# Rounded parts made on GpSimd from one fp32 copy, and ScalarE's copies moved between two exponentials

## The chip, the cores and the metric

The kernel runs on 1 core of one Trainium2 chip. The metric is the device time of one execution in microseconds, the median of several.

## The reference

The input x has 16 images (batch entries) of 512 tokens by 256 features, in fp32. Per image:

```python
x = x + attn(layernorm(x))      # 16 heads of 16, softmax over 512 keys, biases
x = x + (round_fp8(clip(layernorm(x) / input_scale)) * input_scale) @ (w_fp8 * weight_scale).T + bias

# attn(x):
qkv = x @ qkv_w.T + qkv_b
scores = q @ k.T / 4
out = softmax(scores) @ v
return out @ proj_w.T + proj_b
```

## The kernel before, in words

Wherever fp32 accuracy is wanted of the faster fp32r matmuls, an operand is split into a high part (its value rounded to fp32r) and a low part (the value minus the high part), and the product is the sum of three matmuls over the pairs high-high, high-low, low-high. That holds for x (`xnT_p`, the transposed normalised x), q and k (`parts`), the attention output (`oT_p`) and the weights.

The work runs in slots of 32 steps (`STEPS`). In slot u the engines work on four images at once: image u is normalised, transposed and projected; for image u-1 the plain scores and their row maxima are made; for image u-2 the transposed scores, the exponentials and the product with v; for image u-3 the output projection, the second layernorm, the fp8 rounding and the linear layer. `present(n)` says whether image u-n exists. Each engine has its own instruction queue, written out step by step by the same loop, and works it strictly in order; semaphores tie the queues together. Slots 2 to 15 have images u, u-1 and u-2; from slot 3 also image u-3.

On TensorE every step issues: `scores_t(.., 0)` (bank `ps_t[:, 0]`, L455), `scores(.., 1)` (L469), `scores_t(.., 1)`, `scores(.., 0)`, then what the step has extra, and in odd steps eight matmuls with v (`values`, L487). Here t0 and t1 are the two transposed score matmuls, s1 and s0 the plain ones. The extras: v projection at steps 4 and 6 (L380), output projection at 8 and 10 (L406), transposes of x at 12 and 14 (L353), q/k projection at 16, 18, 20 and 22 (L369), transpose of the maxima at 5 and 25 (L390), transposes of the fp8 tile at 26 (L420), linear layer at 28 and 30 (L437). All of the extras use the one PSUM bank `ps_m`; `take_bank` makes TensorE wait for the reader of its last user. The wait of t0 and t1:

```python
if past(2 * STEPS * b + 2 * s + g - 1):
    pe.wait_ge(exp_done, 2 * STEPS * b + 2 * s + g - 1)
```

So t0 of a step needs the first exponential of the step before, and t1 the second. On ScalarE a step has the two exponentials (L566), and behind them the copies that the step's extras need: `copy_v` (L574), `copy_xnT` (L583 rounded, L586 fp32), `copy_oT` (L593) at steps 6 and 24, `copy_qk` (L602 rounded, L603 fp32, both with the bias) and `copy_hqT` (L609). `xnT` is a single buffer of one half of x, so its second fp32 copy waits for `xnT_low` of the first.

VectorE takes the maximum of each step's scores (L684), splits the transposed maxima (L729, L731), does layernorm sums, transposes of the attention output and back (L739, L750), reciprocals, and parts of the fp8 rounding (L765, L771). GpSimd does in this order in a slot: `layernorm_x`, `out_divide(.., 3)`, `low_oT(.., 1)`, `low_xnT(.., 0)` (L903), `out_divide(.., 0)`, `low_xnT(.., 1)`, `layernorm_h` (L939 to L951), `split` 0 and 1 (L924), `out_divide(.., 1)` (L933), `round_fp8` and `add_linear_bias`, `split` 2, `low_oT(.., 0)`, `split` 3, `out_divide(.., 2)`, `add_bias`. The SP queue issues the transfers, among them `stack`: twelve per image and head half, which lay the q and k parts into `qs` and `ks` for the next slot, after `low_ready`.

Of the kernel before, what the change touches and what calls it, by code (L numbers as in the profile page):

```python
# [7 lines left out]
F32R = mybir.dt.float32r  # L8
U32 = mybir.dt.uint32
ALU = mybir.AluOpType  # L10
ACT = mybir.ActivationFunctionType
# [31 lines left out]
PROJECT_V = (4, 6)  # L43
PROJECT_OUT = (8, 10)
TRANSPOSE_X = (12, 14)
PROJECT_QK = (16, 18, 20, 22)
TRANSPOSE_MAX = (25, 5)
TRANSPOSE_HQ = 26
# [3 lines left out]
COPY_OT = (24, 6)  # L52
# [8 lines left out]
def block_kernel(nc, x, qkv_wT, qk_bT, v_bT, proj_wT, proj_b, lin_wT, lin_b, in_scale, w_scale, eye, out):  # L61
# [4 lines left out]
    with ExitStack() as ctx:  # L66
        def sb(name, shape, dt=F32):
            return ctx.enter_context(nc.sbuf_tensor(name, shape, dt))

        def ps(name, shape):  # L70
            return ctx.enter_context(nc.psum_tensor(name, shape, F32))

        def sem(name):
            return ctx.enter_context(nc.semaphore(name))
# [24 lines left out]
        xnT = sb("xnT", [P, S])  # L99
        xnT_p = sb("xnT_p", [P, 2, NC, S], F32R)  # L100
        parts = sb("parts", [P, 2 * NT, 2, S])
# [35 lines left out]
        ps_t = ps("ps_t", [P, 2, S])  # L137
        ps_s = ps("ps_s", [P, 2, 2, S])
        ps_o = ps("ps_o", [P, S])
        ps_m = ps("ps_m", [P, S])  # L140
# [22 lines left out]
        v_done = sem("v_done")  # L163
# [31 lines left out]

        rs1_ready = sem("rs1_ready")
        xn_ready = sem("xn_ready")
        xnT_low = sem("xnT_low")
        oT_low = sem("oT_low")
        low_ready = sem("low_ready")  # L200
        res_ready = sem("res_ready")
        rs2_pow = sem("rs2_pow")
# [7 lines left out]
        def past(count):  # L210

            return not isinstance(count, int) or count > 0

        def run_slots(eng, slot, finish, prepare=None):

            def present(u):
                return lambda behind: 0 <= u - behind < B
            for u in range(NSLOT - 1):  # L220
                slot(u, u % 2, present(u))
                if u == 0 and prepare:
                    prepare()
            finish(B - 1)
# [332 lines left out]
        @block.scalar  # L557
        def _(act):
            def exps(b, s, a):
                n, w = s // 4, s % 4  # L560
                if w == 0 and a == 0 and past(UNITS * b + n - 1):
                    act.wait_ge(pv_done, UNITS * b + n - 1)
                if isinstance(b, int) and b == 0 and s == 0:
                    act.wait_ge(const_v, 9)
                act.wait_ge(st_done, 2 * (STEPS * b + s) + a + 1)
                nc.scalar.activation(pt[n % 2][:, w % 2 + 2 * a, w // 2, :], ps_t[:, a, :], ACT.Exp, scale=SCALE).then_inc(exp_done, 1)  # L566

            def copy_v(b, par, half):
                act.wait_ge(v_done, 2 * b + half + 1)
                if isinstance(b, int) and b == 0:  # L570
                    act.wait_ge(ones, 3)
                if past(UNITS * (b - 1)):
                    act.wait_ge(pv_done, UNITS * (b - 1))
                nc.scalar.copy(vt[par][:, 2 * half:2 * half + 2, :, 0:HD],  # L574
                               ps_m[:].rearrange("p (j h e) -> p j h e", j=2, h=H)).then_inc(v_ready, 1)

            def copy_xnT(b, c):

                bank = ps_t[:, c, :] if isinstance(b, int) and b == 0 else ps_m[:]
                act.wait_ge(xt_done, 2 * b + c + 1)  # L580
                if past(b):
                    act.wait_ge(v_done, 2 * b)
                nc.scalar.copy(xnT_p[:, 0, c, :], bank)  # L583
                if past(2 * b + c):
                    act.wait_ge(xnT_low, 2 * b + c)
                nc.scalar.copy(xnT[:], bank).then_inc(xnT_ready, 1)  # L586

            def copy_oT(b, t):

                act.wait_ge(oT_ready, NT * b + t + 1)  # L590
                if past(b):
                    act.wait_ge(proj_done, 2 * b)
                nc.scalar.copy(oT_p[:, 0, t, :], oT[:]).then_inc(oT_high, 1)  # L593

            def copy_qk(b, par, n):

                t, bias = n // 2, b_qk[:, (n % 2) * NT + n // 2:(n % 2) * NT + n // 2 + 1]
                bank = ps_s[:, n // 2, n % 2, :] if isinstance(b, int) and b == 0 else ps_m[:]
                act.wait_ge(qk_done, 4 * b + n + 1)
                if past(b):  # L600
                    act.wait_ge(stacked[t][1 - par], 96 * (b - 2 + par) + 192)
                nc.scalar.activation(parts[:, n, 0, :].bitcast(F32R), bank, ACT.Identity, bias=bias)  # L602
                nc.scalar.activation(parts[:, n, 1, :], bank, ACT.Identity, bias=bias).then_inc(whole_ready, 1)  # L603

            def copy_hqT(b):
                act.wait_ge(xq_done, b + 1)
                if past(b):
                    act.wait_ge(lin_done, 2 * b)
                nc.scalar.copy(hqT[:].rearrange("p c n -> p (c n)"), ps_m[:].bitcast(BF16)).then_inc(hqT_ready, 1)  # L609

            def slot(u, par, present):
                for s in range(STEPS):
                    if present(2):
                        exps(u - 2, s, 0)
                        exps(u - 2, s, 1)
                    if s == COPY_OT[1] and present(3):
                        copy_oT(u - 3, 1)
                    if s == COPY_OT[0] and present(2):
                        copy_oT(u - 2, 0)
                    if s in PROJECT_V and present(1):  # L620
                        copy_v(u - 1, 1 - par, PROJECT_V.index(s))
                    if s in TRANSPOSE_X and present(0):
                        copy_xnT(u, TRANSPOSE_X.index(s))
                    if s in PROJECT_QK and present(0):
                        copy_qk(u, par, PROJECT_QK.index(s))
                    if s == TRANSPOSE_HQ and present(3):
                        copy_hqT(u - 3)

            def finish(b):
                copy_oT(b, 1)  # L630
                for half in range(2):
                    act.wait_ge(xq_done, b + half + 1)
                    if half == 0:
                        act.wait_ge(lin_done, 2 * b)
                    nc.scalar.copy(hqT[:, :, 2 * half * P:2 * (half + 1) * P],
                                   ps_t[:, half, :].bitcast(BF16)[:, 0:S].rearrange("p (c n) -> p c n", c=NC)
                                   ).then_inc(hqT_ready, 1)


            act.wait_ge(half_set, 1)  # L640
            nc.scalar.activation(table[:], half_neg[:, 0:1], ACT.Exp)
            act.wait_ge(ident_in, 32)
            run_slots(act, slot, finish)

        @block.vector
# [236 lines left out]
        def _(pool):  # L882
# [16 lines left out]
            def low_xnT(b, c):  # L899
                pool.wait_ge(xnT_ready, 2 * b + c + 1)  # L900
                if past(b):
                    pool.wait_ge(v_done, 2 * b)
                pool.tensor_tensor(xnT_p[:, 1, c, :], xnT[:], xnT_p[:, 0, c, :].bitcast(F32),  # L903
                                   ALU.subtract).then_inc(xnT_low, 1)

# [15 lines left out]
            def split(b, n):  # L921

                pool.wait_ge(whole_ready, 4 * b + n + 1)
                pool.tensor_tensor(parts[:, n, 1, :], parts[:, n, 1, :], parts[:, n, 0, :],  # L924
                                   ALU.subtract).then_inc(low_ready, 1)

# [41 lines left out]
            def slot(u, par, present):  # L968
# [6 lines left out]
                if present(0) and later:  # L975
                    low_xnT(u, 0)
                if present(2):
                    out_divide(u - 2, 0)
                if present(0) and later:
                    low_xnT(u, 1)  # L980
                if present(3):
                    layernorm_h(u - 3)
                if present(0) and later:
                    split(u, 0)
                    split(u, 1)
# [5 lines left out]
                if present(0) and later:  # L991
                    split(u, 2)
# [59 lines left out]
```

## Time and profile before

| | |
|---|---|
| median of 3 runs | 1080.2 us (1075.93 to 1088.58) |
| the profiled execution | 1080.5 us, of which span 1078.7 us |
| TensorE busy | 975.6 us, 90% |
| VectorE busy | 857.8 us, 80% |
| ScalarE busy | 707.2 us, 66% |
| GpSimd busy | 465.6 us, 43% |
| granted TensorE clock, mean | 0.951 |

The span runs from the first instruction to the last. Busy shares are means over the whole span; matmuls are pipelined, and their ends in the profile are modelled, so starts are the safer reading. The granted clock is a share of full speed, 2.4 GHz. Times in the rows below count from the start of the span.

### The profile page before, as it was taken

The numbers are of one execution on the slowest core, as the hardware profiler recorded it, in microseconds if no ns is written. First come the engines' busy times: TensorE is split into PE (matmuls) and PEld (weight loads), VectorE is DVE, ScalarE is ACT, GpSimd is POOL, SyncE is SP. The second block draws the span as 40 slices with busy tenths as digits, with TensorE's granted clock in tenths as the row PEclk, the third lists the DMA queues.
The fourth block names the chain that finished last, engine by engine and source line by source line (L and its number), as shares of the span: only waits on it lengthen the run. The fifth ranks groups of instructions, "written<-read, shape, count | busy, mean of one in ns | idle before, by whom it ended". The sixth has DMA issues, their size and how long they took to land.

```text
span 1078.7 us, 16257 instructions
## 1 busy us (share of the span) xinstructions
PE 975.6 (90%) x5796; PEld 451.3 (42%) x5796; DVE 857.8 (80%) x1186; ACT 707.2 (66%) x1299; POOL 465.6 (43%) x443
## 2 busy tenths in 40 slices
PE   3487999999999999999999999999999999998894
PEld 2243334454444434444444444344444434443333
DVE  3576788888987888898988888888989888888216
ACT  3023767777685777777686777777686777766650
POOL 3121234627272463717264453727273553524242
PEclk9666999999998999999999999999999999999966
DMA  4928181745646083665638182645647181741000
GB/s 137 124 35 88 39 110 30 104 76 81 99 56 103 29 107 65 85 95 73 107 43 124 28 107 58 94 85 80 99 53 107 26 106 29 101 59 41 2 29 30
DMA packets 44288, 79.39 MB, mean 74 GB/s; under 512 B 9904, under 2 KB 13104, under 8 KB 44208
## 3 DMA queue, kind: packets, MB, share of 16 engines
q1 hardware_dynamic: 44208, 78.36, 48.5%
q8 instruction: 46, 0.75, 0.4%
q14 instruction: 34, 0.28, 0.1%
HBM read 18.42 MB, written 8.39 MB: 25 GB/s over the span
## 4 chain that ended last, share of the span: by engine, by line
PE 74%; ACT 14%; DVE 6%; issue 2%; DMA 2%; SPq 1%; POOL 1%; ACTq 0%; DVEq 0%; POOLq 0%
PE ps_t L455 27%; PE ps_o L487 18%; PE ps_m L369 9%; ACT pt L566 6%; PE ps_m L380 5%; PE ps_m L406 4%; PE ps_s L469 4%; ACT parts L602 4%; ACT parts L603 3%; DVE mx L684 3%; PE ps_m L437 2%; PE ps_m L353 2%; DMA ks<-parts 1%; PE ps_m L420 1%; DVE nm L700 1%
## 5 line engine op out<-in xcount | busy, mean ns | idle before, releaser
L684 DVE TENSOR_REDUCE mx<-ps_s 128x2 f32<-128x1024 f32 x512 | 616.6, 1215 | 112.4 <-PE ps_s L469 108.8
L566 ACT ACTIVATE pt<-ps_t 128x512 f32<-128x512 f32 x1024 | 558.9, 600 | 213.8 <-PE ps_t L455 205.6
L455 PE MATMUL ps_t<-qs,ks 50*128 50x512 f32 x1024 | 424.4, 474 | 44.3 <-ACT pt L566 39.1
L469 PE MATMUL ps_s<-ks,qs 48*128 48x512 f32 x1024 | 413.1, 482 | 23.6 <-DVE mx L684 12.1
L455 PEld LDWEIGHTS ps_t<-qs,ks 50*128 50x128 f32 x1024 | 168.5, 187 | 386.1 <-ACT pt L566 307.2
L487 PE MATMUL ps_o<-pt,vt 128*32 128x512 f32 x2048 | 277.7, 615 | 0.2 <-ACT pt L566 0.2
L469 PEld LDWEIGHTS ps_s<-ks,qs 48*128 48x128 f32 x1024 | 162.8, 190 | 37.6 <-DVE mx L684 19.4
L903 POOL TENSOR_TENSOR xnT_p<-xnT,xnT_p 128x512 fp32r<-128x512 f32 x30 | 38.3, 1277 | 212.7 <-ACT xnT L586 212.7
L933 POOL TENSOR_TENSOR on<-ot,rden 128x256 f32<-128x256 f32 x63 | 39.4, 626 | 174.8 <-DVE rden L743 174.8
L369 PE MATMUL ps_m<-xnT_p,wqkv_p 128*128 128x512 f32 x360 | 103.2, 423 | 1.5 <-POOL xnT_p L903 0.8
L924 POOL TENSOR_TENSOR parts<-parts 128x512 f32<-128x512 f32 x60 | 76.6, 1277 | 37.4 <-ACT parts L603 37.4
L602 ACT ACTIVATE parts<-ps_m,b_qk 128x512 fp32r<-128x512 f32 x60 | 41.3, 688 | 65.5 <-PE ps_m L369 65.5
L369 PEld LDWEIGHTS ps_m<-xnT_p,wqkv_p 128*128 128x128 f32 x360 | 65.3, 195 | 28.9 <-issue 14.9
L487 PEld LDWEIGHTS ps_o<-pt,vt 128*32 128x32 f32 x2048 | 40.6, 108 | 78.6 <-issue 73.5
L910 POOL TENSOR_TENSOR oT_p<-oT,oT_p 128x512 fp32r<-128x512 f32 x31 | 39.6, 1279 | 75.3 <-ACT oT_p L593 75.3
L739 DVE STREAM_TRANSPOSE ot<-ps_o 128x512 f32<-128x512 f32 x64 | 45.3, 707 | 29.6 <-PE ps_o L487 29.6
L380 PE MATMUL ps_m<-wqkv_p,xnT_p 128*128 128x256 f32 x384 | 56.6, 299 | 0.0
L380 PEld LDWEIGHTS ps_m<-wqkv_p,xnT_p 128*128 128x128 f32 x384 | 50.0, 200 | 12.3 <-issue 11.9
L406 PE MATMUL ps_m<-wproj_p,oT_p 128*128 128x256 f32 x360 | 50.6, 290 | 0.0
L406 PEld LDWEIGHTS ps_m<-wproj_p,oT_p 128*128 128x128 f32 x360 | 44.5, 189 | 10.8 <-issue 10.8
L918 POOL TENSOR_TENSOR xres<-xres,b_proj 128x1024 f32<-128x1024 f32 x16 | 38.4, 2399 | 20.8 <-DMA xres<-in_x 20.8
L574 ACT COPY vt<-ps_m 128x512 f32<-128x512 f32 x32 | 18.8, 587 | 41.2 <-PE ps_m L380 41.2
(94 smaller groups left out, 761.5 us busy)
## 6 DMA issues: line engine op xcount, KB each, us to landing
qs<-parts SPq DMA_DIRECT2D x192, 128.0 KB, 6.5
ks<-parts SPq DMA_DIRECT2D x192, 128.0 KB, 7.0
xin<-in_x SPq DMA_DIRECT2D x16, 512.0 KB, 4.5
xres<-in_x SPq DMA_DIRECT2D x16, 512.0 KB, 3.8
out<-h SPq DMA_DIRECT2D x15, 512.0 KB, 9.0
qs<-nmax SPq DMA_DIRECT2D x128, 8.0 KB, 4.6
pt<-in_qkv_wT SPq DMA_DIRECT2D x1, 768.0 KB, 6.6
out<-h SPq DMA_DIRECT2D x2, 256.0 KB, 2.0
```

The source lines that it names most:

```text
L369: last = nc.tensor.matmul(bank, wqkv_p[:, pw, c, first:first + P], xnT_p[:, px, c, :], start=(m == 0 and c == 0), stop=(m == 2 and c == NC ...
L380: last = nc.tensor.matmul(ps_m[:, j * D:(j + 1) * D], xnT_p[:, px, c, tok], wqkv_p[:, pw, c, 2 * D:3 * D], start=(m == 0 and c == 0), stop ...
L406: last = nc.tensor.matmul(bank[:, j * D:(j + 1) * D], oT_p[:, px, t, tok], wproj_p[:, pw, t, :], start=(m == 0 and t == 0), stop=(m == 2 a ...
L455: nc.tensor.matmul(ps_t[:, g, :], ks[par][rows, slot, keys], qs[par][rows, slot, :], start=True, stop=True).then_inc(st_done, 1)
L469: done = nc.tensor.matmul(ps_s[:, s % 2, g, :], qs[par][rows, slot, queries], ks[par][rows, slot, :], start=True, stop=True)
L487: last = nc.tensor.matmul(ps_o[32 * i:32 * i + VW, :], vt[par][:, 2 * kp + a, head, :], pt[n % 2][:, i, a, :], start=(kp == 0 and a == 0), ...
L566: nc.scalar.activation(pt[n % 2][:, w % 2 + 2 * a, w // 2, :], ps_t[:, a, :], ACT.Exp, scale=SCALE).then_inc(exp_done, 1)
L602: nc.scalar.activation(parts[:, n, 0, :].bitcast(F32R), bank, ACT.Identity, bias=bias)
L684: dve.tensor_reduce(mx[:, t, :, s % (STEPS // 2)], ps_s[:, s % 2, :, :], AX_X, ALU.max).then_inc(max_done, 1)
L739: dve.transpose(ot[:].rearrange("p a c -> p (a c)"), ps_o[:]).then_inc(ot_ready, 1)
L910: pool.tensor_tensor(oT_p[:, 1, t, :], oT[:], oT_p[:, 0, t, :].bitcast(F32), ALU.subtract).then_inc(oT_low, 1)
L924: pool.tensor_tensor(parts[:, n, 1, :], parts[:, n, 1, :], parts[:, n, 0, :], ALU.subtract).then_inc(low_ready, 1)
```

## The change

For images 1 to 15, ScalarE copies each bank once, in fp32. GpSimd makes the rounded part from that copy by a `tensor_copy` and then subtracts as before; between the two it waits for its own copy by the new semaphores `xnT_high` and `high_ready` (which count only from image 1 on, thence the `b - 1`). The wait for `v_done`, which protects `xnT_p`, stands on GpSimd alone. Image 0, whose parts are split on VectorE, keeps both ScalarE copies. And ScalarE's queue is reordered: all copies of step s-1 (v, x, oT, q and k, hqT) stand between the first and the second exponential of step s.

```diff
--- before.py
+++ after.py
@@ -195,8 +195,10 @@
 
         rs1_ready = sem("rs1_ready")
         xn_ready = sem("xn_ready")
+        xnT_high = sem("xnT_high")
         xnT_low = sem("xnT_low")
         oT_low = sem("oT_low")
+        high_ready = sem("high_ready")
         low_ready = sem("low_ready")
         res_ready = sem("res_ready")
         rs2_pow = sem("rs2_pow")
@@ -576,11 +578,10 @@
 
             def copy_xnT(b, c):
 
-                bank = ps_t[:, c, :] if isinstance(b, int) and b == 0 else ps_m[:]
+                bank = ps_t[:, c, :] if b == 0 else ps_m[:]
                 act.wait_ge(xt_done, 2 * b + c + 1)
-                if past(b):
-                    act.wait_ge(v_done, 2 * b)
-                nc.scalar.copy(xnT_p[:, 0, c, :], bank)
+                if b == 0:
+                    nc.scalar.copy(xnT_p[:, 0, c, :], bank)
                 if past(2 * b + c):
                     act.wait_ge(xnT_low, 2 * b + c)
                 nc.scalar.copy(xnT[:], bank).then_inc(xnT_ready, 1)
@@ -599,7 +600,8 @@
                 act.wait_ge(qk_done, 4 * b + n + 1)
                 if past(b):
                     act.wait_ge(stacked[t][1 - par], 96 * (b - 2 + par) + 192)
-                nc.scalar.activation(parts[:, n, 0, :].bitcast(F32R), bank, ACT.Identity, bias=bias)
+                if b == 0:
+                    nc.scalar.activation(parts[:, n, 0, :].bitcast(F32R), bank, ACT.Identity, bias=bias)
                 nc.scalar.activation(parts[:, n, 1, :], bank, ACT.Identity, bias=bias).then_inc(whole_ready, 1)
 
             def copy_hqT(b):
@@ -608,23 +610,27 @@
                     act.wait_ge(lin_done, 2 * b)
                 nc.scalar.copy(hqT[:].rearrange("p c n -> p (c n)"), ps_m[:].bitcast(BF16)).then_inc(hqT_ready, 1)
 
+            def copies(u, par, present, s):
+                if s == COPY_OT[1] and present(3):
+                    copy_oT(u - 3, 1)
+                if s == COPY_OT[0] and present(2):
+                    copy_oT(u - 2, 0)
+                if s in PROJECT_V and present(1):
+                    copy_v(u - 1, 1 - par, PROJECT_V.index(s))
+                if s in TRANSPOSE_X and present(0):
+                    copy_xnT(u, TRANSPOSE_X.index(s))
+                if s in PROJECT_QK and present(0):
+                    copy_qk(u, par, PROJECT_QK.index(s))
+                if s == TRANSPOSE_HQ and present(3):
+                    copy_hqT(u - 3)
+
             def slot(u, par, present):
                 for s in range(STEPS):
                     if present(2):
                         exps(u - 2, s, 0)
+                    copies(u, par, present, s - 1)
+                    if present(2):
                         exps(u - 2, s, 1)
-                    if s == COPY_OT[1] and present(3):
-                        copy_oT(u - 3, 1)
-                    if s == COPY_OT[0] and present(2):
-                        copy_oT(u - 2, 0)
-                    if s in PROJECT_V and present(1):
-                        copy_v(u - 1, 1 - par, PROJECT_V.index(s))
-                    if s in TRANSPOSE_X and present(0):
-                        copy_xnT(u, TRANSPOSE_X.index(s))
-                    if s in PROJECT_QK and present(0):
-                        copy_qk(u, par, PROJECT_QK.index(s))
-                    if s == TRANSPOSE_HQ and present(3):
-                        copy_hqT(u - 3)
 
             def finish(b):
                 copy_oT(b, 1)
@@ -900,6 +906,8 @@
                 pool.wait_ge(xnT_ready, 2 * b + c + 1)
                 if past(b):
                     pool.wait_ge(v_done, 2 * b)
+                pool.tensor_copy(xnT_p[:, 0, c, :], xnT[:]).then_inc(xnT_high, 1)
+                pool.wait_ge(xnT_high, 2 * (b - 1) + c + 1)
                 pool.tensor_tensor(xnT_p[:, 1, c, :], xnT[:], xnT_p[:, 0, c, :].bitcast(F32),
                                    ALU.subtract).then_inc(xnT_low, 1)
 
@@ -921,6 +929,8 @@
             def split(b, n):
 
                 pool.wait_ge(whole_ready, 4 * b + n + 1)
+                pool.tensor_copy(parts[:, n, 0, :].bitcast(F32R), parts[:, n, 1, :]).then_inc(high_ready, 1)
+                pool.wait_ge(high_ready, 4 * (b - 1) + n + 1)
                 pool.tensor_tensor(parts[:, n, 1, :], parts[:, n, 1, :], parts[:, n, 0, :],
                                    ALU.subtract).then_inc(low_ready, 1)
 
```

## Rows read from the trace of the kernel before

**Rows 1.** Stretches: busy us of each engine, granted clock, DMA share, GB/s

```profile
466.00:526.00 60.00, 57.95 (x364) 26.69 (x362) 52.08 (x73) 43.94 (x81) 29.63 (x28) 1.00 0.54 81
```

**Rows 2.** List of waits: waiter, releaser, us in total, times, longest

```profile
PEld ps_m L390 <- ACT vt L574: 6.9, 15, 0.7
```

**Rows 3.** Timeline, all engines, steps 5 to 7: start, length, engine, instruction

```profile
466.05 0.50 PE L455 MATMUL ps_t<-qs,ks 50*128 50x512 f32 x1
...
466.16 0.59 ACT L574 COPY vt<-ps_m 128x512 f32<-128x512 f32 x1 [0.66 <-PE ps_m L380]
...
466.64 1.09 ACT L566 ACTIVATE pt<-ps_t 128x512 f32<-128x512 f32 x2
466.80 0.09 PEld L390 LDWEIGHTS ps_m<-ident,mx 128*32 128x32 f32 x1 [0.45 <-ACT vt L574]
...
468.01 0.50 PE L455 MATMUL ps_t<-qs,ks 50*128 50x512 f32 x1
...
468.54 1.09 ACT L566 ACTIVATE pt<-ps_t 128x512 f32<-128x512 f32 x2 [0.81 <-PE ps_t L455]
...
469.51 0.62 ACT L593 CAST oT_p<-oT 128x512 fp32r<-128x512 f32 x1
...
470.29 0.50 PE L455 MATMUL ps_t<-qs,ks 50*128 50x512 f32 x1
```

**Rows 4.** Timeline of TensorE's matmuls, steps 8 to 28

```profile
471.96 0.50 PE L455 MATMUL ps_t<-qs,ks 50*128 50x512 f32 x1
...
472.62 1.69 PE L406 MATMUL ps_m<-wproj_p,oT_p 128*128 128x256 f32 x12
...
480.52 0.66 PE L353 MATMUL ps_m<-ident,xn 128*128 128x128 f32 x4
...
483.98 0.66 PE L353 MATMUL ps_m<-ident,xn 128*128 128x128 f32 x4
...
487.24 1.64 PE L369 MATMUL ps_m<-xnT_p,wqkv_p 128*128 128x512 f32 x6
488.81 0.50 PE L455 MATMUL ps_t<-qs,ks 50*128 50x512 f32 x1
...
490.72 0.50 PE L455 MATMUL ps_t<-qs,ks 50*128 50x512 f32 x1 [0.19 <-ACT pt L566]
...
491.21 0.50 PE L455 MATMUL ps_t<-qs,ks 50*128 50x512 f32 x1
...
491.65 1.67 PE L369 MATMUL ps_m<-xnT_p,wqkv_p 128*128 128x512 f32 x6
...
508.59 0.50 PE L455 MATMUL ps_t<-qs,ks 50*128 50x512 f32 x1
...
511.38 1.21 PE L437 MATMUL ps_m<-wlin_p,hqT 128*128 128x256 f32 x8
```

**Rows 5.** Timeline of ScalarE, the same slot

```profile
485.15 0.59 ACT L586 COPY xnT<-ps_m 128x512 f32<-128x512 f32 x1
...
489.50 0.68 ACT L603 ACTIVATE parts<-ps_m,b_qk 128x512 f32<-128x512 f32 x1
490.07 2.28 ACT L566 ACTIVATE pt<-ps_t 128x512 f32<-128x512 f32 x4
...
508.88 1.02 ACT L609 CAST hqT<-ps_m 128x1024 fp32r<-128x1024 bf16 x1
```

**Rows 6.** Timeline of GpSimd, the same slot

```profile
485.82 1.28 POOL L903 TENSOR_TENSOR xnT_p<-xnT,xnT_p 128x512 fp32r<-128x512 f32 x1 [1.39 <-ACT xnT L586]
...
496.27 0.62 POOL L933 TENSOR_TENSOR on<-ot,rden 128x256 f32<-128x256 f32 x1 [0.30 <-DVE rden L743]
```

**Rows 7.** Timeline of VectorE, the same slot

```profile
501.77 0.70 DVE L750 STREAM_TRANSPOSE oT<-on 128x512 f32<-128x512 f32 x1
```

**Rows 8.** Groups by form: busy us, mean ns of one, idle before

```profile
L951 POOL TENSOR_SCALAR hn<-hn 128x1024 f32<-128x1024 f32 x15 | 15.6, 1040 | 2.9 <-POOL hn L946 2.9
```

## The prediction

> **What bounds the kernel now.** I read the busy shares first. In a steady stretch of 60 us TensorE is busy 57.95 us, VectorE 52.08, ScalarE 43.94 and GpSimd 29.63, at a granted clock of 1.00 (the 2.4 GHz level) [rows 1]. So a microsecond counts if TensorE stands still for it, and ScalarE's busy time counts only where TensorE waits for its result. The profiled execution took 1080.5 us with a span of 1078.7, 0.3 us over the median of 1080.2; all sums are made on 1080.5.
>
> A slot of 32 steps takes about 60 us. The next view is the timeline of one slot. Every step runs t0 with s1, then t1 with s0 (t is the transposed score matmul of a head group, s the plain one; the two pass through the array together), then the step's extra matmuls; odd steps add eight value matmuls. In flow the two pairs take 0.66 us (471.96 to 472.62) [rows 4]. t0 of the next step needs the first exponential of this step, t1 the second. I use five constants from rows: an exponential starts 0.55 us after its pair (468.01 to 468.54, 0.53; other steps 0.59) [rows 3]; the next ScalarE instruction starts 0.49 after an exponential (468.54 to 469.51, two exponentials, 0.97) [rows 3]; a copy of v, x or oT also holds ScalarE 0.49 (466.16 to 466.64, 0.48) [rows 3], a copy of q or k 0.57 (489.50 to 490.07) [rows 5]; a pair that waits for an exponential starts 0.65 after that exponential (490.07 to 490.72) [rows 4, 5]; and behind a pair that waited the next matmul comes 0.44 later instead of 0.33 (491.21 to 491.65) [rows 4].
>
> **The change part by part.** Each copy moves from behind the two exponentials of step s to between the two of step s+1. ScalarE works in order, so the copy now starts 0.55 + 0.49 = 1.04 us after t0 of the next step at the earliest, and the second exponential stands behind it. From the loops: 14 slots have q, k and x beside exponentials (slots 2 to 15), 14 the copy of oT with v (3 to 16), 15 the v copy with the transpose of the maxima (2 to 16), 15 the hqT copy (3 to 17).
>
> (a) The v copy of step 4. The next user of the one bank ps_m is the transpose of the maxima at step 5, and it waits for this copy already in 15 slots, 6.9 us in all [rows 2]: t0 at 466.05, copy at 466.16, transpose at 466.80, that is 0.64 after the copy's start and 0.75 after t0 [rows 3]. After the change the copy starts 1.04 after t0 and the transpose 1.68. Nothing covers it: the value matmuls are queued behind the transpose. Loss 0.93 x 15 = 14.0 us. The VectorE split of the maxima and the four row transfers on SP's queue move with it; they are wanted at step 16, some 20 us on, so this costs nothing more.
>
> (b) At step 7 two copies now stand between the exponentials, oT (formerly before t0, at 469.51) and v. With t0 at 470.29 as zero the second exponential starts at 0.55 + 0.49 + 0.49 + 0.49 = 2.02, so t1 of step 8 starts at 2.67 and the output projection at 3.11. It now starts at 472.62, 2.33 after that t0 [rows 3, 4]. Loss 0.78 x 14 = 10.9. GpSimd's low part of oT ends near the same moment (copy end 1.66, 1.28 more) and adds nothing. Where one such copy stands alone (v at step 5, x at 13 and 15, oT at 25), the next t1 could start at 2.18, and in flow it comes at 1.67 (470.29 to 471.96) plus half of 0.66, 2.00 [rows 3, 4]; beside the steps' own longer work (transposes, the waiting t1) I take nothing, with 0.18 each as the other end.
>
> (c) Transposed x. The q/k matmuls of step 16 need the low part of x's second half. From the second transpose (483.98) to them (487.24) are 3.26 us [rows 4], through the fp32 copy at 485.15 [rows 5] and GpSimd at 485.82 [rows 6]. After: 0.58 to t0 (the transposes are 0.66 long [rows 4], and the next pair starts 0.08 before their modelled end), 0.55 to the exponential, 0.49 to the copy, 0.67 to GpSimd (485.15 to 485.82), the new GpSimd copy, 0.20 for GpSimd's wait on its own write (its clipping waits for itself in the same way, 2.9 us in 15 times [rows 8]), 1.28 for the subtraction, and 0.14 to TensorE (487.10 to 487.24) [rows 4, 6]. The new copy has no row. Nearest below is the single-input instruction on 1024 columns, 1.04 us, half of which is 0.52 [rows 8]; nearest above the two-input subtraction on 512 columns, 1.28 [rows 6]. A saving is excluded, since the subtraction remains. A copy reads one input, so I take 0.65, near the lower row, as an estimate: half of 1.04 and something for the start of an instruction. Sum 4.56, 1.30 more. The first transpose to the second (480.52 to 483.98, 3.46 [rows 4]) shrinks by 0.29, because one copy instead of two lets t0 and t1 of step 14 flow. Loss 1.01 x 14 = 14.1; with 0.52 it is 12.3, with 1.28 it is 23.
>
> The Trainium skill (GPSIMD Engine Reference, Performance versus the Vector engine) gives 769 ns for a tight loop over 512 elements, and advises VectorE for elementwise work. No run here shows that copy; with 0.77 term (c) would be 15.8 and the total 1.7 higher.
>
> (d) The four copies of q and k. Now the first exponential of the next step waits for both copies. From t0 (488.81) to the next q/k matmuls (491.65) are 2.84 us, with t0 of step 18 waiting and both pairs slow [rows 4]. After: second exponential at 0.55 + 0.49 + 0.57 = 1.61, t1 at 2.26, the matmuls at 2.70. ScalarE loses an instruction of 0.68 each time, but TensorE gains only 0.14: the wait goes from t0 to t1. Four per slot, 0.56 x 14 = 7.8 us gained. The longer split on GpSimd (0.65 + 0.20 more for each) feeds the stacking transfers, whose data are wanted in the next slot, and delays what is queued behind it there: the division, the fp8 rounding and the bias. The division ends at 496.89 and VectorE wants it at 501.77 [rows 6, 7]: 4.9 us of cover, against some 1.3 + 0.85 + 0.85 = 3.0 more ahead of it.
>
> (e) The hqT copy is 1.02 us long [rows 5]; less the 0.12 by which a shorter copy overlaps with its successor (0.68 long, 0.57 to the next) it holds ScalarE 0.90. After t0 of step 27 the second exponential starts at 0.55 + 0.49 + 0.90 = 1.94, t1 of step 28 at 2.59, the linear matmuls at 3.03, against 2.79 now (508.59 to 511.38) [rows 4]. Loss 0.24 x 15 = 3.6.
>
> The waits for v_done move from ScalarE to GpSimd, where they stand already: nothing. Slot 1 has no exponentials and loses one copy but gains a longer GpSimd chain: nothing within 0.5 us. Sum: 14.0 + 10.9 + 14.1 - 7.8 + 3.6 = 34.8, so 1080.5 + 34.8 = 1115 us.
>
> **The rivals.** First, faster: the pairs and the value matmuls hide every copy, and TensorE runs in flow. Then (a), (b), (c) and (e) are nothing, and (d) gains 2.84 - 2.33 = 0.51 four times (2.33 being the flow from t0 to the next extra matmuls, 470.29 to 472.62 [rows 3, 4]), with the 0.29 of (c): 2.33 x 14 = 33, giving 1048 us. For it speaks that ScalarE is free 16 us of 60; against it the 15 waits at the transpose of the maxima, which come from when ScalarE gets to a copy, with time to spare on it. Chance 0.09.
>
> Second, little difference: a late t1 costs nothing because s0 and the queued matmuls go ahead. Then (b) and (e) vanish and (d) rises to 0.51 four times, 28.6 us, against 14.0 + 14.1 for (a) and (c): 1080. Against it: s0 is queued behind t1. Chance 0.12.
>
> Third, slower still: the GpSimd queue becomes late. The low part of x and two splits stand ahead of the second division, which VectorE waits for at step 22 before its maxima. With the new copy at 1.28 and 0.20 of waiting this is 3 x 1.48 = 4.4 us, of 4.9 us of cover. If the later start of the x copy (0.4 us) and a copy slightly over 1.28 carry it past 4.9, VectorE, the scores and TensorE lose what is over. At 1 us a slot, with (c) at 23, this gives 1115 + 9 + 14 = 1138. Chance 0.10.
>
> Fourth, the copies don't bear on the time (each wait named is covered by another that the rows don't tell apart): 1080, chance 0.04. That leaves 0.65 for the forecast, with a range of its own from 1104 (hand-offs 0.1 us shorter at five places, 0.52 for the copy) to 1128 (1.28 for the copy, and 0.18 at two lone copies).
>
> **How the numbers follow.** About 1% is what a measurement of this kernel tells from no change. Slower by over 1%: 0.65 + 0.10 and a quarter of the second rival, 0.78. Within 1%: the rest of the second and the fourth, less 0.02 that falls below, 0.11. Faster: 0.11. For the range I leave out the first rival (0.09), half of the second (0.06) and half of the third (0.05): 1078 to 1130.
>
> **What would show it.** In the changed kernel's timeline: the transpose of the maxima at step 5 starts about 1.7 us after t0, and its wait for the v copy comes to about 20 us in all; t1 of step 8 waits for an exponential; the q/k matmuls of step 16 wait for GpSimd's low part, by over 0.7 us in 14 slots; between q/k groups are 4.3 instead of 4.4 us; ScalarE is busy about 60 us less over the span. The prediction is wrong if TensorE's waits for ScalarE at t1 are no longer than before, or if GpSimd's copy is well under 0.5 us.

## The result and the profile after

The changed kernel takes 1115.25 us (median of 4, 1109.88 to 1124.95) against 1082.18 before (median of 4). The ratio is 1.0315, 95% interval 1.0219 to 1.0412: slower. The forecast was 1115. The profiled execution took 1124.95 us, the slowest of its four, with a span of 1123.2; its mean granted clock, 0.936, is the lowest of the four (0.948, 0.958 and 0.949 in the others), and the last section tells where its time went. Executions that come out over 1.5% above the fastest of their kernel, at a lower mean clock, are left out of every ratio; the profile of e6 below is of such a one.

Busy time of each engine in the changed kernel's page, against 707.2 us of ScalarE and 465.6 of GpSimd before:

```profile
PE 984.9 (88%) x5796; PEld 454.7 (40%) x5796; DVE 854.6 (76%) x1186; ACT 667.5 (59%) x1209; POOL 524.2 (47%) x533
```

ScalarE lost 90 instructions and 40 us, GpSimd gained 90 and 59 us. Neither sum says anything of the end. The list of waits does:

```profile
ACT pt L568 <- PE ps_t L457: 356.4, 351, 16.2
...
PE ps_t L457 <- ACT pt L568: 37.6, 95, 0.7
...
PEld ps_m L392 <- ACT vt L576: 20.5, 15, 1.5
...
PE ps_m L371 <- POOL xnT_p L911: 17.1, 15, 1.4
...
PE ps_m L392 <- ACT vt L576: 13.7, 15, 0.9
```

ScalarE now waits 356 us for the transposed scores (206 before). The transpose of the maxima (L392, formerly L390) has its wait for the v copy grown from 6.9 us [rows 2] to 20.5, and the q/k matmuls (L371) have a new one for GpSimd, 17.1 us in 15 times, where the whole of the run before had 0.8 in one. TensorE's own waits for exponentials, t0's and t1's together, are about what they were:

```profile
PE ps_t L455 <- ACT pt L566: 39.1, 120, 0.8
```

What changed is where they stand, as the next rows show.

The timeline of all engines in steps 5, 7 and 8 of one slot of the changed kernel, which answers to [rows 3]:

```profile
535.88 0.50 PE L457 MATMUL ps_t<-qs,ks 50*128 50x512 f32 x1
...
536.41 0.60 ACT L568 ACTIVATE pt<-ps_t 128x512 f32<-128x512 f32 x1 [1.08 <-PE ps_t L457]
536.90 0.58 ACT L576 COPY vt<-ps_m 128x512 f32<-128x512 f32 x1
537.37 0.62 ACT L568 ACTIVATE pt<-ps_t 128x512 f32<-128x512 f32 x1
...
537.54 0.28 PE L392 MATMUL ps_m<-ident,mx 128*32 128x128 f32 x1 [0.93 <-ACT vt L576]
...
540.98 0.50 PE L457 MATMUL ps_t<-qs,ks 50*128 50x512 f32 x1
...
542.01 0.61 ACT L594 CAST oT_p<-oT 128x512 fp32r<-128x512 f32 x1
542.52 0.59 ACT L576 COPY vt<-ps_m 128x512 f32<-128x512 f32 x1
...
542.70 1.27 POOL L918 TENSOR_TENSOR oT_p<-oT,oT_p 128x512 fp32r<-128x512 f32 x1 [7.06 <-ACT oT_p L594]
...
543.00 1.79 ACT L568 ACTIVATE pt<-ps_t 128x512 f32<-128x512 f32 x3
...
543.66 0.49 PE L457 MATMUL ps_t<-qs,ks 50*128 50x512 f32 x1 [0.51 <-ACT pt L568]
...
544.11 1.66 PE L408 MATMUL ps_m<-wproj_p,oT_p 128*128 128x256 f32 x12
```

The copy starts 1.02 us after t0 (535.88 to 536.90) and the transpose 1.66 after it, where it was 0.75. Two copies hold the second exponential of step 7 until 543.00, and t1 of step 8 stands still for 0.51. GpSimd's low part of oT ends at 543.97, and the output projection starts at 544.11. TensorE's matmuls in the slot before it, as in [rows 4]:

```profile
491.91 0.66 PE L355 MATMUL ps_m<-ident,xn 128*128 128x128 f32 x4
...
496.27 1.64 PE L371 MATMUL ps_m<-xnT_p,wqkv_p 128*128 128x512 f32 x6 [1.12 <-POOL xnT_p L911]
497.84 0.50 PE L457 MATMUL ps_t<-qs,ks 50*128 50x512 f32 x1
...
499.50 0.50 PE L457 MATMUL ps_t<-qs,ks 50*128 50x512 f32 x1
...
500.09 0.50 PE L457 MATMUL ps_t<-qs,ks 50*128 50x512 f32 x1
...
500.52 1.67 PE L371 MATMUL ps_m<-xnT_p,wqkv_p 128*128 128x512 f32 x6
...
516.98 0.49 PE L457 MATMUL ps_t<-qs,ks 50*128 50x512 f32 x1
...
520.00 1.21 PE L439 MATMUL ps_m<-wlin_p,hqT 128*128 128x256 f32 x8
```

From the second transpose to the q/k matmuls are 4.36 us (3.26 before), from t0 to the next q/k matmuls 2.68 (2.84 before): t0 at 499.50 no longer waits, t1 at 500.09 does, 0.59 behind it. From t0 of step 27 to the linear matmuls are 3.02 us (516.98 to 520.00), where they were 2.79. GpSimd's part of the 4.36 us:

```profile
494.17 0.61 POOL L909 CAST xnT_p<-xnT 128x512 fp32r<-128x512 f32 x1 [0.62 <-ACT xnT L587]
494.86 1.27 POOL L911 TENSOR_TENSOR xnT_p<-xnT,xnT_p 128x512 fp32r<-128x512 f32 x1
```

The new copy takes 0.61 us, and the subtraction starts 0.69 after the copy's start.

From such starts I took the interval between neighbouring extras of a slot, and of each the median over the 13 slots that have all four images. This table is the measure for all that follows. In its head stand the steps: 4>5 is the time in us from the start of step 4's extra to that of step 5's, and 30>4 ends in the next slot.

```
                  4>5  5>6  6>8  12>14 14>16 16>18 18>20 20>22 22>25 26>28 30>4  slot
before            2.31 1.88 3.95 3.46  3.27  4.39  4.42  4.42  5.67  3.33  9.75  60.10
whole change      3.23 1.88 4.70 3.17  4.36  4.25  4.28  4.28  5.47  3.57  9.72  62.12
e1 move only      3.23 1.88 4.70 3.67  4.17  4.83  4.85  4.84  6.03  3.57  9.78  64.76
e2 GpSimd only    2.31 1.87 3.94 3.16  3.61  3.88  3.93  3.92  5.42  3.32  9.72  58.32
e3 v behind       2.31 1.87 4.81 3.17  4.36  4.25  4.28  4.28  5.47  3.57  9.72  61.30
e4 values first   3.23 0.97 4.75 3.17  4.36  4.25  4.28  4.28  5.47  3.57  9.72  61.28
e5 double q/k     3.23 1.88 4.70 3.18  4.36  4.25  4.28  4.28  5.47  3.57  9.71  62.16
e6 q/k, x between 2.36 1.88 3.90 3.17  4.35  4.24  4.27  4.28  5.45  3.32  9.75  60.22
e7 double x       3.23 1.88 4.69 3.17  5.24  5.40  4.27  4.28  5.45  3.57  9.72  64.14
e8 e2 + e4        3.27 0.97 4.30 3.16  3.61  3.89  3.92  3.92  5.42  3.33  9.74  58.77
e9 q/k only       2.31 1.87 3.94 3.45  3.27  3.89  3.92  3.92  5.42  3.33  9.73  58.29
e10 x behind      3.23 1.88 4.69 3.16  3.61  4.24  4.27  4.28  5.45  3.57  9.72  61.34
```

(Left out are 8>10, 10>12, 25>26 and 28>30, which stay within 0.03 of 3.95, 3.95, 1.88 and 3.47. The slot is the sum of all, with those left out.)

### The profile page after: what moved, and what is told of

It reads as the page before. It is cut to its first block, busy times and chain, and to the rows that moved or that the text cites. A ratio compares the mean times of both kernels' runs of the same rounds, so it can differ in the third digit from the quotient of the medians.

```text
span 1123.2 us, 16257 instructions
## 1 busy us (share of the span) xinstructions
PE 984.9 (88%) x5796; PEld 454.7 (40%) x5796; DVE 854.6 (76%) x1186; ACT 667.5 (59%) x1209; POOL 524.2 (47%) x533
## 4 chain that ended last, share of the span: by engine, by line
PE 65%; ACT 16%; issue 7%; DVE 5%; POOL 3%; DMA 2%; SPq 1%; ACTq 0%; POOLq 0%; DVEq 0%
PE ps_t L457 24%; PE ps_o L489 14%; PE ps_m L371 8%; ACT pt L568 8%; PE ps_m L382 5%; PE ps_m L408 4%; ACT parts L605 4%; PE ps_s L471 3%; PE ps_m L439 2%; POOL xnT_p L911 2%; DVE mx L690 2%; PE ps_m L355 2%; ACT vt L576 1%; SPq L282 1%; ACT hqT L611 1%
## 5 line engine op out<-in xcount | busy, mean ns | idle before, releaser
L568 ACT ACTIVATE pt<-ps_t 128x512 f32<-128x512 f32 x1024 | 578.9, 598 | 367.8 <-PE ps_t L457 356.4
L457 PE MATMUL ps_t<-qs,ks 50*128 50x512 f32 x1024 | 431.3, 484 | 49.4 <-ACT pt L568 37.6
L471 PE MATMUL ps_s<-ks,qs 48*128 48x512 f32 x1024 | 420.8, 485 | 26.0 <-DVE mx L690 14.0
L457 PEld LDWEIGHTS ps_t<-qs,ks 50*128 50x128 f32 x1024 | 172.1, 190 | 399.4 <-ACT pt L568 313.8
L489 PE MATMUL ps_o<-pt,vt 128*32 128x512 f32 x2048 | 284.0, 628 | 0.2 <-ACT pt L568 0.2
L471 PEld LDWEIGHTS ps_s<-ks,qs 48*128 48x128 f32 x1024 | 165.3, 191 | 39.2 <-DVE mx L690 20.7
L371 PE MATMUL ps_m<-xnT_p,wqkv_p 128*128 128x512 f32 x360 | 101.5, 417 | 17.2 <-POOL xnT_p L911 17.1
L909 POOL CAST xnT_p<-xnT 128x512 fp32r<-128x512 f32 x30 | 18.3, 612 | 198.1 <-ACT xnT L587 198.1
L934 POOL TENSOR_TENSOR parts<-parts 128x512 f32<-128x512 f32 x60 | 83.2, 1387 | 4.9
L371 PEld LDWEIGHTS ps_m<-xnT_p,wqkv_p 128*128 128x128 f32 x360 | 64.2, 192 | 44.4 <-issue 31.8
L605 ACT ACTIVATE parts<-ps_m,b_qk 128x512 f32<-128x512 f32 x60 | 40.9, 682 | 11.4 <-PE ps_m L371 11.4
L932 POOL CAST parts<-parts 128x512 fp32r<-128x512 f32 x60 | 36.7, 612 | 17.0 <-ACT parts L605 16.8
```

The lines of the kernel that those rows point to most:

```text
L371: last = nc.tensor.matmul(bank, wqkv_p[:, pw, c, first:first + P], xnT_p[:, px, c, :], start=(m == 0 and c == 0), stop=(m == 2 and c == NC ...
L457: nc.tensor.matmul(ps_t[:, g, :], ks[par][rows, slot, keys], qs[par][rows, slot, :], start=True, stop=True).then_inc(st_done, 1)
L471: done = nc.tensor.matmul(ps_s[:, s % 2, g, :], qs[par][rows, slot, queries], ks[par][rows, slot, :], start=True, stop=True)
L489: last = nc.tensor.matmul(ps_o[32 * i:32 * i + VW, :], vt[par][:, 2 * kp + a, head, :], pt[n % 2][:, i, a, :], start=(kp == 0 and a == 0), ...
```

## The experiments

Theory P: the place between the exponentials costs, and the halved copying gains. Theory G: GpSimd's longer chain, or its conflicts with VectorE, is the cost. Ratios are to the kernel before.

**The two halves of the change.** e1 takes only the new order of ScalarE's queue into the kernel before:

```diff
+                    copies(u, par, present, s - 1)
+                    if present(2):
                         exps(u - 2, s, 1)
-                    if s == COPY_OT[1] and present(3):
-                        copy_oT(u - 3, 1)
...
```

> Only the reordering of ScalarE's queue, with both ScalarE copies (rounded and fp32) kept and GpSimd as before. Theory P (the place between the exponentials costs, the halved copying gains): terms (a), (b) and (e) as in the change, 14.0 + 10.9 + 3.6; four pairs of q/k copies now hold the second exponential until 0.55 + 0.49 + 0.57 + 0.57 = 2.18, t1 at 2.83, the next q/k matmuls at 3.27 instead of 2.84 after t0: 0.43 x 4 x 14 = 24; x some 1.1 x 14 = 16. Sum about 68: 1150 us, ratio 1.063. Theory G (GpSimd's longer chain and its conflicts with VectorE are the cost): without them nearly the time of before, at most 1.01.

Measured: 1139.14 us, ratio 1.0478 (1.0414 to 1.0542). Slower, and by more than the whole change: theory G is out as the main cost (what GpSimd's copy does cost, 0.34 us a slot, e10 shows). The intervals are close to what was expected: the three between q/k groups grew by 0.44, 0.43 and 0.42 (0.43 expected), the two of x together by 1.11 (1.1 expected), and 4.66 us x 14 slots would be 65. The timed runs give some 52; the last section shows where such a difference can lie.

e2 takes only the other half, the changed kernel with the old order:

```diff
-                    copies(u, par, present, s - 1)
-                    if present(2):
                         exps(u - 2, s, 1)
+                    if s == COPY_OT[1] and present(3):
+                        copy_oT(u - 3, 1)
...
```

> Only the work moved to GpSimd; the copies stand behind both exponentials as before. Theory P: (a), (b), (e) are nothing. One q/k copy ends in time for t0 of the next even step to flow: 2.33 instead of 2.84, 0.51 x 4 x 14 = 28.6 us gained. x: low part 0.2 later (a GpSimd copy of 0.61 for a ScalarE copy of 0.48), 0.29 gained at step 14: 1 us gained. About 1052 us, ratio 0.973. Theory G: 1.02 to 1.03, as the whole change.

Measured: 1050.59 us, ratio 0.9675 (0.9627 to 0.9723), the fastest of all versions, 34 us under the kernel before. TensorE's matmuls in it:

```profile
474.40 1.67 PE L371 MATMUL ps_m<-xnT_p,wqkv_p 128*128 128x512 f32 x6
476.01 0.50 PE L457 MATMUL ps_t<-qs,ks 50*128 50x512 f32 x1
...
477.66 0.50 PE L457 MATMUL ps_t<-qs,ks 50*128 50x512 f32 x1
...
478.33 1.66 PE L371 MATMUL ps_m<-xnT_p,wqkv_p 128*128 128x512 f32 x6
```

and ScalarE at the same place:

```profile
476.11 0.69 ACT L605 ACTIVATE parts<-ps_m,b_qk 128x512 f32<-128x512 f32 x1 [0.76 <-PE ps_m L371]
476.70 1.08 ACT L568 ACTIVATE pt<-ps_t 128x512 f32<-128x512 f32 x2
```

The copy starts 0.10 after t0 (476.01), in the time in which ScalarE would wait for t0's result anyway. The first exponential ends before t0 at 477.66, the second at 477.78, and all flows: 2.32 us from t0 to the next q/k matmuls instead of 2.84. The new order throws this free place away.

e9 leaves of e2 only q and k (x has both ScalarE copies again and no GpSimd copy):

```diff
-                if b == 0:
-                    nc.scalar.copy(xnT_p[:, 0, c, :], bank)
+                nc.scalar.copy(xnT_p[:, 0, c, :], bank)
...
-                pool.tensor_copy(xnT_p[:, 0, c, :], xnT[:]).then_inc(xnT_high, 1)
-                pool.wait_ge(xnT_high, 2 * (b - 1) + c + 1)
```

> Of the change only q and k: their rounded parts on GpSimd, one ScalarE copy, placed behind both exponentials; x as in the kernel before. By the slot intervals: (d) 0.51 x 3 plus 0.25 at the last, x 6.73 us from the first transpose to the q/k matmuls where the run with x on GpSimd too has 6.77. So all the gain is q and k's: within 2 us of the GpSimd part alone, ratio 0.967. If x's part carried some of that gain: 0.975 or more.

Measured: 1052.23 us, 0.9696 (0.9635 to 0.9757). x's part is even (12>16 is 6.72 against 6.77 with it); the gain is q and k's.

**Each copy put back.** Three runs put copies of the changed kernel behind both exponentials again. In e3 those of v:

```diff
                         exps(u - 2, s, 1)
+                    if s in PROJECT_V and present(1):
+                        copy_v(u - 1, 1 - par, PROJECT_V.index(s))
```

> The changed kernel with the copies of v alone put back behind both exponentials. Theory P: term (a) is gone, 0.93 x 15 = 14.0, and of (b) only oT between the exponentials of step 7 behind a v copy remains, output projection at 2.68 after t0 instead of 3.11: 0.43 x 14 = 6.0. 20 us less than the whole change: 1095 us, ratio 1.012. Theory G: 1.031 as the whole change, since GpSimd's work is the same.

Measured: 1105.40 us, 1.0194 (1.0118 to 1.027). Term (a) went away whole (4>5 is 2.31 again), but (b) did not: 6>8 is 4.81, where about 4.3 was expected. Its timeline:

```profile
537.54 0.62 ACT L594 CAST oT_p<-oT 128x512 fp32r<-128x512 f32 x1
...
538.24 1.28 POOL L918 TENSOR_TENSOR oT_p<-oT,oT_p 128x512 fp32r<-128x512 f32 x1 [8.38 <-ACT oT_p L594]
...
539.67 1.67 PE L408 MATMUL ps_m<-wproj_p,oT_p 128*128 128x256 f32 x12 [0.45 <-POOL oT_p L918]
```

With t1 early, the output projection waits for the low part of oT: the move of oT's copy alone makes that chain end at the same time. Term (b) had two causes side by side, and taking one away gives nothing. That the late t1 alone would hold the projection as long is read from the rows of the changed kernel (543.66 + 0.44 = 544.10); no run takes away the low part's delay and leaves t1's.

In e10 the two lines moved are those of x:

```diff
                         exps(u - 2, s, 1)
+                    if s in TRANSPOSE_X and present(0):
+                        copy_xnT(u, TRANSPOSE_X.index(s))
```

> The changed kernel with the copies of x alone put back behind both exponentials (still one ScalarE copy, the rounding on GpSimd). Term (c) splits into the place and the GpSimd copy: with the place undone the chain from the second transpose to the q/k matmuls is 3.61 us as in the GpSimd part alone, where the whole change has 4.36: 0.75 x 14 = 10.5 us less than the whole change, ratio 1.021. If GpSimd's copy, not the place, makes (c): 1.031.

Measured: 1110.51 us, 1.0206 (1.0128 to 1.0284). 14>16 falls from 4.36 to 3.61, so of the 1.09 us that it grew, 0.75 are the place and 0.34 the GpSimd copy in place of ScalarE's.

In e6 they are those of oT (shown), v and hqT:

```diff
                         exps(u - 2, s, 1)
+                    if s == COPY_OT[1] and present(3):
+                        copy_oT(u - 3, 1)
...
```

> The changed kernel with the copies of v, oT and hqT behind both exponentials again, only q, k and x between them. Theory P: (a), (b), (e) are gone; (c) 0.80 and (d) -0.64 per slot remain as the whole change's trace has them, 0.2 x 14 = 2 us: 1.002 of before. Against it: if between the exponentials is a good place for q, k and x and only the other copies suffered from it, this keeps the gain of the run with the GpSimd part alone: 0.968.

Measured: 1074.25 us, 0.9911 (0.9874 to 0.9949). Slots of 60.22 against 60.10 before: with q, k and x between the exponentials nothing of e2's gain is left in them. The time lies between the two expectations (1.002 and 0.968), and its interval excludes both; it is about 1% under what the slots say, which the last section takes up.

**Is TensorE's wait the price?** e4 swaps two items in TensorE's order of the changed kernel:

```diff
-                    if s == TRANSPOSE_MAX[1] and present(2):
-                        transpose_max(u, 1, 2)
...
                         if n < 0 and present(3):
                             values(u - 3, 1 - par, UNITS - 1, s // 2 % 2)
+                    if s == TRANSPOSE_MAX[1] and present(2):
+                        transpose_max(u, 1, 2)
```

> The changed kernel with one thing else: on TensorE the transpose of the maxima stands behind the eight value matmuls of its step instead of ahead of them. If the transpose's wait for the v copy (0.91 us in 15 slots) is what (a) costs, 1.0 us of value matmuls now covers it and 13.7 us come back: 1101 us, ratio 1.018, and the wait of that transpose for the v copy is under 2 us in total. If that wait only takes the place of a later one, nothing: 1.031.

Measured: 1103.01 us, 1.0165 (1.0103 to 1.0227), as expected. The transpose itself now starts later by design, so 4>5 says nothing here; from step 4 to step 6 are 4.20 us, 0.91 less than in the changed kernel and as many as before (4.19). The eight value matmuls cover the wait, and term (a) is shown. Its list of waits has no row any more for the matmuls of the transpose, only for its weight load (TensorE then still works on the value matmuls):

```profile
PEld ps_m L392 <- ACT vt L576: 12.9, 15, 1.2
```

e8 joins e4's edit to e2.

> A version meant to be fastest: the GpSimd part alone (copies behind both exponentials), and the transpose of the maxima behind the value matmuls of its step. From the median intervals of the GpSimd part's trace the transpose's wait for the v copy is about 0.1 us a slot, so 1 to 2 us: 1049 us, ratio 0.966. A later split of the maxima could hold VectorE's next maximum up by up to 1 us a slot, which would show as 0.975 or more.

Measured: 1064.13 us, 0.9829 (0.9734 to 0.9924), 13 us slower than e2. There was nothing to cover in e2, and the swap delays VectorE, though not at its next maximum, as feared: its split of the maxima stands ahead of its transpose of the output, and ScalarE's oT copy now waits for that in 15 slots. From the lists of waits of e8 and of e2:

```profile
ACT oT_p L594 <- DVE oT L752: 16.3, 15, 4.3
```

```profile
ACT oT_p L594 <- DVE oT L752: 4.3, 1, 4.3
```

6>8 grows from 3.94 to 4.30. The same edit is a gain in one kernel and a loss in the other. The slots give 6 us of the 13; most of the rest lies behind the last full slot (see the last section).

**GpSimd's queue.** e5 and e7 make GpSimd's rounding copies of the changed kernel twice, e5 those of q and k, e7 those of x (e7's edit is shown):

```diff
                 pool.tensor_copy(xnT_p[:, 0, c, :], xnT[:]).then_inc(xnT_high, 1)
-                pool.wait_ge(xnT_high, 2 * (b - 1) + c + 1)
+                pool.wait_ge(xnT_high, 2 * (2 * (b - 1) + c) + 1)
+                pool.tensor_copy(xnT_p[:, 0, c, :], xnT[:]).then_inc(xnT_high, 1)
+                pool.wait_ge(xnT_high, 2 * (2 * (b - 1) + c) + 2)
```

> The changed kernel, with GpSimd's rounding copy of q and k made twice (the second waits for the first). By its trace a copy with its hand-off is 0.69 us, so GpSimd gets 0.69 x 4 = 2.8 us more in each of 14 slots. Theory P: nothing on the path; the second division still comes over 1 us before VectorE wants it, and the rounding before TensorE's step 26. As the whole change: 1.031, at most 3 us more. The third rival (GpSimd's queue is already late): at least 1 us a slot of it shows, ratio 1.045 or more.

Measured: 1113.94 us, 1.0293 (1.0188 to 1.0399), slots of 62.16 against 62.12: 2.8 us more on GpSimd per slot cost nothing. The third rival, a late GpSimd queue, is out.

> The changed kernel, with GpSimd's rounding copy of x made twice. Theory P, term (c): the chain from the second transpose to the q/k matmuls is bare, so the added 0.69 shows in full, and the second fp32 copy starts up to 0.2 later since it waits for the first half's low part: 0.69 to 0.89 x 14 = 10 to 12 us over the whole change, ratio 1.041. If the wait at the q/k matmuls has another cause that ends near the same time, less than 3 us: 1.033.

Measured: 1145.61 us, 1.0594 (1.0477 to 1.0711), some 30 us over the whole change where 10 to 12 were expected. 14>16 grew by 0.88, as expected: 0.69 for the copy and 0.19 for the later ScalarE copy. That is 12 us, and shows the chain of (c) bare. More is lost in 16>18, 5.40 instead of 4.25, in which nothing was changed. The row of its q/k matmuls:

```profile
504.64 2.61 PE L371 MATMUL ps_m<-xnT_p,wqkv_p 128*128 128x512 f32 x6 [1.45 <-POOL xnT_p L913]
```

and its stretches there, with the granted clock behind the busy times:

```profile
504.00:505.00 1.00, 0.36 (x2) 0.35 (x3) 0.94 (x1) 0.00 (x0) 1.00 (x2) 0.99 0.00 0
505.00:506.00 1.00, 1.00 (x4) 0.81 (x3) 0.00 (x0) 0.00 (x0) 0.72 (x2) 0.50 0.09 16
506.00:507.00 1.00, 1.00 (x3) 0.42 (x2) 0.00 (x0) 0.00 (x0) 0.86 (x2) 0.50 0.00 0
507.00:508.00 1.00, 1.00 (x5) 0.50 (x4) 0.00 (x0) 0.00 (x0) 1.00 (x3) 0.50 0.00 0
508.00:509.00 1.00, 1.00 (x10) 0.16 (x8) 0.53 (x1) 0.99 (x2) 0.81 (x2) 0.81 0.00 0
```

After a stop of 1.45 us TensorE ran some 3.4 us at 0.50, the 1.2 GHz level; the six matmuls took 2.61 us instead of 1.64. It did so in 8 of 14 slots (16>18 there 5.39 to 5.76, in the others 4.23 to 4.25), 10 us in all. With the 12 this is about the difference of the two profiled executions, 21.0 us (1145.97 and 1124.95; the full slots are 24.9 us longer, with their ends, and the rest 3.9 shorter). The medians differ by 9 more, because the changed kernel's profiled execution lies 9.7 over its median and that of e7 lies on it (1145.61). The changed kernel with its stop of 1.12 us at the same place kept its clock in all slots.

## Why the prediction was right

In the slots with all four images the whole change costs 2.02 us; the terms of the prediction gave 2.40. The mechanism was right term by term; the size of (c) was furthest off.

- (a), 0.93: measured 0.92 in 4>5, and shown as the place's cost by e3 and as TensorE's wait by e4.
- (b), 0.78: measured 0.75. Right in size, incomplete in cause: I let the low part of oT "add nothing". That is so while t1 is late, but it ends level with t1, so that taking away t1's wait alone gains nothing (e3).
- (c), 1.01: measured 1.09 - 0.29 = 0.80. The 0.29 at step 14 was exact. The mis-sized term is GpSimd's, 0.16 of the 0.21: copy 0.65 estimated and 0.61 measured, its wait on its own write 0.20 and 0.08. The figure of 769 ns that the Trainium skill gives for a loop over 512 elements (GPSIMD Engine Reference, Performance versus the Vector engine) does not hold for this copy: 612 ns on average over 30, as these groups of the changed kernel's lines show:

```profile
L909 POOL CAST xnT_p<-xnT 128x512 fp32r<-128x512 f32 x30 | 18.3, 612 | 198.1 <-ACT xnT L587 198.1
...
L932 POOL CAST parts<-parts 128x512 fp32r<-128x512 f32 x60 | 36.7, 612 | 17.0 <-ACT parts L605 16.8
```

- (d), a gain of 0.56: measured 0.14 three times and 0.20 at 22>25, 0.62. That a halved copy should gain so little because the wait goes from t0 to t1 was the least obvious step; e2 shows what the old place would have given, 0.49 to 0.51 three times and 0.25 at 22>25.
- (e), 0.24: measured 0.24 in 26>28.

The bounds that the prediction gives its own forecast, 1104 to 1128, don't quite come out of what they name: five hand-offs 0.1 us shorter and 0.13 less for the copy take 8.8 us off 1115, to 1106, and 0.63 more for the copy with 0.18 at two copies adds 13.9, to 1129. The range of 1078 to 1130 doesn't hang on it.

The slots' 2.02 x 14 = 28 us and the parts of (a) and (e) in the slots at the ends, about 1, make 1.027 of the time, inside the measured interval. That its centre, 33 us, agrees so well with the 35 is in part luck: some 4 us that no term foresaw and that lie within the noise of the timed runs stood for some 6 of terms set too high.

The first rival (TensorE flows, 1048 us) is refuted for this kernel and is nearly what e2 is, 1050.6: it needs the copies where they were. The second (a late t1 costs nothing) fails on the 0.51 us at 543.66. Beside the time, one check given ahead failed: ScalarE's busy time fell by 40 us and not 60 (90 copies of 0.58 to 0.69 less, but the exponentials, now broken up by copies, are counted with 20 us more, 578.9 against 558.9).

## What to carry to other kernels

Ahead of moving an instruction in an engine's queue, ask what the engine does at its present place: here a copy of q or k stood where ScalarE had to wait for TensorE anyway and cost TensorE nothing, and the new place was on the path from the first exponential to the second. Test a change of two parts in its halves; one half of this was worth 34 us, and the other ate all of it and nearly as much again. A cover made for one wait (e4) is a loss where the wait is not there (e8).

## What the runs showed of the hardware

**A very small VectorE instruction can wait for a long GpSimd one.** VectorE's rows at the end of a slot of the changed kernel:

```profile
523.50 2.36 DVE L706 TENSOR_SCALAR nm<-mv 128x4 f32<-128x4 f32 x1
525.77 0.16 DVE L707 TENSOR_SCALAR ve<-mv 128x4 f32<-128x4 f32 x1
```

GpSimd's and TensorE's there:

```profile
523.44 2.39 POOL L926 TENSOR_TENSOR xres<-xres,b_proj 128x1024 f32<-128x1024 f32 x1 [2.60 <-DMA xres<-in_x]
```

```profile
527.20 0.50 PE L471 MATMUL ps_s<-ks,qs 48*128 48x512 f32 x2 [0.44 <-DVE mx L690]
...
528.90 0.51 PE L471 MATMUL ps_s<-ks,qs 48*128 48x512 f32 x2 [0.90 <-DVE mx L690]
```

Four columns take 0.17 us (the median of 16) when GpSimd is idle, and 2.36 when the bias addition has started 0.06 earlier: they end at 525.86, the addition at 525.83. In one slot it was the next instruction, L707, that met the addition, with 2.38 us. By the Trainium skill (SBUF — State Buffer, Who interferes with whom) a VectorE tensor_scalar in a two-port mode and a GpSimd instruction lock each other out for a whole instruction, whoever is first. The trace agrees for GpSimd being first; which mode VectorE's instruction had, no view shows. The maxima come late, and 30>4 grows by 1.1 us; in two slots TensorE's stops were followed by a fall of the granted clock, and it grew by 3.2 and 3.9:

```profile
587.00:591.00 4.00, 3.60 (x25) 1.82 (x23) 4.00 (x5) 2.35 (x5) 3.58 (x3) 1.00 0.18 57
591.00:595.00 4.00, 3.15 (x17) 0.95 (x15) 3.30 (x3) 1.92 (x4) 1.64 (x4) 0.81 1.07 118
595.00:599.00 4.00, 3.74 (x16) 1.27 (x16) 2.83 (x3) 1.93 (x4) 0.00 (x0) 0.50 1.08 113
```

Whether they meet depends on when a transfer lands (the addition starts behind its wait for `in_x`). In the profiled run of the changed kernel slots so stretched add 9.4 us in all over 9.72 each, in that of the kernel before 7.0 (13 of its 16 such instructions took 0.9 us or more, and every one of over 2 us cost at least 0.95), in e2, e5, e8 and e9 none.

**Most of what the full slots don't explain lies outside them.** The profiled execution of the changed kernel is 44.5 us longer than that of the kernel before (spans of 1123.2 and 1078.7). The 13 full slots give 26.2 of it by their medians and 3.5 by stretched slots. The stretch ahead of them is 3.1 longer, and the one behind the last of them 11.7; some 3 us of these two are the terms (a) to (e) in the slots there. These are the rows of the last stretch, of the changed kernel and of the one before:

```profile
979.03:1123.20 144.17, 115.08 (x601) 50.14 (x599) 72.27 (x121) 71.89 (x131) 43.59 (x40) 0.78 0.12 28
```

```profile
946.27:1078.70 132.43, 105.23 (x601) 46.69 (x599) 72.14 (x121) 71.23 (x131) 43.57 (x40) 0.87 0.13 31
```

The same 601 matmuls take 9.9 us more of TensorE's time, at a granted clock of 0.78 instead of 0.87: 62 us of this stretch ran at 0.50, against 34. In the same way 6.7 of the 13 us between e8 and e2 lie behind the last full slot (57 and 38 us at 0.50).

The timed runs have no traces, but each has its mean clock, and from that and its span the time at 0.50 follows. By the medians, e1, e2, e6 and e9 spent 20 to 33 us less at it than the kernel before in the same rounds, and it is these four that stand 8 to 13 us lower against it than their slots say. e3, e4, e5, e8 and e10 spent 1 to 12 us more at it and stand level with their slots or up to 5 us above (e7, with its falls inside the slots, is left out). As 0.50 costs at most half of the time spent at it, this is of the size of the differences. Why one execution spends more time at 0.50 outside the full slots than another, no run shows.

**The clock can fall behind short stops.** In e7 the granted clock fell behind a stop of 1.45 us, and of the changed kernel's in the stretch from 587 on behind stops of 0.40 and 0.85 us close together; behind the changed kernel's stops of 1.12 us, and behind the 0.44 and 0.90 at 527.20 and 528.90, it stayed at 1.00. So the length of a stop alone does not tell whether it falls: 1.45 was followed by a fall in some slots and not in others, and so were the pairs of about 0.4 and 0.9. A fall cost 1.1 to 1.5 us in e7 and some 2 to 3 at the slots' ends, on top of the stop.
